# Unread matmuls in TensorE's waits, and another order around the end of the second attention

## The chip, the cores and the metric

The kernel runs on one NeuronCore of a Trainium2 chip. The metric is the time of one execution on the device, in microseconds (us). Five engines work from their own instruction lists and wait for one another through semaphores: TensorE (PE, matrix products; its weight loads are listed apart as PEld), VectorE (DVE), ScalarE (ACT), GpSimd (POOL) and SyncE (SP, which here only starts transfers). TensorE's results go to PSUM, eight banks of 128 x 512 float32 numbers, from which VectorE and ScalarE read them.

## What is computed

Eight sequences of 128 tokens with 128 features pass through two layers. Each layer has a cross-attention to a context of the same shape and a feed-forward part, both added to the running x; each normalises its input.

```python
# layer 0: cross-attention, 16 heads of 8, with relative positions
energy = q k^T + q rel^T;  attn = softmax(energy / sqrt(8));  x += (attn v) Wo + bo
# layer 0: feed-forward with fake-quantised activations and weights (352 hidden)
xq = quant(ln(x)); h = quant(silu(xq Wg^T) * (xq Wu^T)); x += h Wd^T
# layer 1: cross-attention, 16 heads of 8
probs = softmax(q k^T / sqrt(8));  x += (probs v) Wo^T + bo
# layer 1: feed-forward, itself two blocks ("local layers") on z = ln(x)
h = shift_token(z); q, k, v = split(h @ wqkv)            # 8 heads of 64
q, k = rotary_xpos(l2norm(q) * qs, l2norm(k) * ks)
z += local_attention(q, k, v) @ wo                       # masked, window of 64
h = ln(shift_token(z)); a, g = split(h @ w1 + b1); z += (a * gelu(g)) @ w2 + b2
out = x + z
```

Here `shift_token` moves the upper 64 features one token on.

## The kernel before

Everything stays on the chip: 8 tiles of 128 tokens (n = 0 to 7), one per sequence. Each engine's program is a Python function that writes instructions in a fixed order; nothing reorders them later. So an instruction that waits for a semaphore holds back all that stands behind it on its engine.

**End of the first feed-forward part.** `spread_max(1)` (TensorE, L432 and L434) spreads the largest hidden value. VectorE scales and rounds the hidden values (L881, L883), ScalarE writes them as bf16 `hq` (L1334), and TensorE multiplies them by the down weights (L453) in two halves of four tiles. VectorE adds the result to x (`add_feed_forward(c)`, L1049 and L1053), takes mean and variance (`moments`, L770 to L775), and after a logarithm and an exponential on ScalarE (`norm_root`) three steps of Newton and the rows Y (`normalise`, L788 to L783). TensorE's `queries1(h)` turns four rows (L462) and projects them (L465).

**Second attention.** It runs in 16 units u, two per tile, each with eight heads. TensorE: `scores1` (L478, in PSUM banks 0 to 3), `turn1` (transposes of the probabilities, L491), `weigh1` (L503). VectorE: maximum (L1077) and subtraction (L1081). ScalarE: exponential (L1444) and two copies of the turned probabilities (L1441). After two units ScalarE takes the weighed values (`take_batch`), TensorE turns them back (`turn_back`, L517, bank 7) and VectorE divides them (`divide_batch`, L1068 and L1070). For each half of four tiles TensorE turns the outputs and projects them (`turn_second_o` L292, `project_second_o` L298), VectorE adds them to x (`add_projection(1, h)`, L866) and takes moments. Then z is normalised into `Z`, turned by TensorE (`turn_z(h)`, L525, bank 7) and copied into the shifted `hT` by ScalarE (L1347, L1348).

**Local layers.** A loop of 16 passes, one per tile and layer, that is started while the attention ends. `qkv(i)` (L549) makes queries, keys and values as three matmuls in banks 0, 1 and 2, with one semaphore at the end. ScalarE squares (L1361) and copies values (L1366). VectorE's `rotate(i)` (L1105 to L1117) applies the rotary tables and sums the squares, `unit_norm(i)` scales (to L1123). TensorE's `turn_qk` (L562), `score` and `shift` (both through L251: band and scores, then the negative maximum), `turn_p` (L607), `weigh` (L616), `turn_o` (L591) and `project_o` (L597) follow. VectorE's `largest(i)` (L1130) gives the maximum, ScalarE's `exponential(i)` (L1390) the probabilities.

The semaphores that carry the work around the change are `less_max` (subtraction done), `exp1`, `z_in` (rows of z), `zT` (`hT` filled), `rope` (turned queries and keys scaled), `kT`, `lmax`, `lexp`.

## Time and profile before

| | |
|---|---|
| three runs | 458.27, 458.41, 460.68 us (median 458.41) |
| profiled execution, its own time | 460.31 us |
| its span, first to last instruction | 458.5 us |
| mean granted clock of TensorE | 0.918 of 2.4 GHz |
| busy: TensorE, VectorE, ScalarE | 382.0, 356.7, 235.5 us |

Busy shares alone do not say what a stage waits for. In the timeline a row is a start, a duration, an engine with its line, what it writes and reads, how many instructions are merged, and in brackets how long the engine had been idle and what ended that. The clock is either 1.2 or 2.4 GHz (0.50 or 1.00 of full); a stretch with a number between contains both.

### The profile page before, as it was taken

The numbers are of one execution on the slowest core, as the hardware profiler recorded it, in microseconds if no ns is written. First come the engines' busy times: TensorE is split into PE (matmuls) and PEld (weight loads), VectorE is DVE, ScalarE is ACT, GpSimd is POOL, SyncE is SP. The second block draws the span as 40 slices with busy tenths as digits, with TensorE's granted clock in tenths as the row PEclk, the third lists the DMA queues.
The fourth block names the chain that finished last, engine by engine and source line by source line (L and its number), as shares of the span: only waits on it lengthen the run. The fifth ranks groups of instructions, "written<-read, shape, count | busy, mean of one in ns | idle before, by whom it ended". The sixth has DMA issues, their size and how long they took to land.

```text
span 458.5 us, 10020 instructions
## 1 busy us (share of the span) xinstructions
PE 382.0 (83%) x4101; PEld 280.6 (61%) x4101; DVE 356.7 (78%) x721; ACT 235.5 (51%) x432; POOL 21.0 (5%) x30
## 2 busy tenths in 40 slices
PE   3898899998453689988777998999999899997966
PEld 1597788876312235554455676867767676776854
DVE  5999998997798679775877779878796978774542
ACT  1744444442454157765443455747656565754541
POOL 2000020000020110000000000000000001010110
PEclk9999999999755579997888999999999999997997
DMA  8500000000000000000000000000000000000000
GB/s 338 249 5 3 20 21 4 3 4 1 0 0 2 0 0 1 2 1 0 1 1 1 0 1 1 2 1 0 1 0 2 1 1 1 1 0 2 24 1 23
DMA packets 1773, 8.29 MB, mean 18 GB/s; under 512 B 192, under 2 KB 448, under 8 KB 1472
## 3 DMA queue, kind: packets, MB, share of 16 engines
q1 hardware_dynamic: 1728, 7.65, 4.2%
q8 instruction: 33, 0.54, 0.5%
q14 instruction: 12, 0.10, 0.1%
HBM read 7.12 MB, written 0.52 MB: 17 GB/s over the span
## 4 chain that ended last, share of the span: by engine, by line
PE 51%; DVE 33%; ACT 10%; issue 5%; DMA 1%; DVEq 0%; ACTq 0%
PE ps L251 12%; PE ps L549 9%; DVE blk L825 5%; PE ps L649 5%; PE ps L616 3%; PE ps L661 3%; PE ps L491 2%; PE ps L478 2%; PE ps L607 2%; DVE blk L1114 2%; DVE blk L1105 2%; PE ps L597 2%; DVE ss L1115 2%; ACT blk L1361 2%; ACT PT L1444 2%
## 5 line engine op out<-in xcount | busy, mean ns | idle before, releaser
L549 PE MATMUL ps<-w_f,full 128*128 128x512 f32 x96 | 45.8, 614 | 0.7 <-DVE blk L1109 0.7
L1293 ACT ACTIVATE St<-ps 128x512 bf16<-128x512 f32 x32 | 19.1, 597 | 44.9 <-PE ps L251 44.9
L1105 DVE TENSOR_TENSOR blk<-ps,tabs 128x1024 f32<-128x1024 f32 x16 | 19.6, 1224 | 28.9 <-ACT blk L1361 28.9
L1361 ACT ACTIVATE blk<-ps 128x1024 f32<-128x1024 f32 x16 | 16.4, 1027 | 30.5 <-PE ps L549 30.5
L616 PEld LDWEIGHTS ps<-blk,PT 128*128 128x128 f32 x256 | 30.3, 192 | 1.6
L616 PE MATMUL ps<-blk,PT 128*128 128x65 f32 x256 | 31.3, 275 | 0.0
L549 PEld LDWEIGHTS ps<-w_f,full 128*128 128x128 f32 x96 | 18.5, 200 | 18.8 <-issue 17.7
L251 PEld LDWEIGHTS ps<-blk,st 128*128 128x128 bf16 x768 | 26.7, 98 | 3.8
L251 PE MATMUL ps<-blk,rel 128*128 128x64 bf16 x768 | 27.6, 193 | 0.0
L251 PE MATMUL ps<-blk,st 128*128 128x64 bf16 x768 | 27.6, 193 | 0.0
L607 PE MATMUL ps<-const,PT 128*128 128x128 f32 x128 | 17.9, 285 | 9.3 <-ACT blk L1384 9.3
L1390 ACT ACTIVATE PT<-ps 128x1024 f32<-128x1024 f32 x16 | 16.3, 1019 | 17.3 <-PE ps L251 17.3
L649 PE MATMUL ps<-YT,w_f 128*128 128x256 f32 (+1 forms) x96 | 24.5, 408 | 0.7 <-ACT YT L1414 0.7
L966 DVE TENSOR_REDUCE mneg<-ps 128x4 bf16<-128x512 bf16 x32 | 22.0, 686 | 3.5 <-PE ps L349 3.3
L251 PEld LDWEIGHTS ps<-blk,rel 128*128 128x128 bf16 x768 | 24.6, 98 | 0.0
L562 PEld LDWEIGHTS ps<-const,blk 128*128 128x128 f32 x128 | 16.2, 151 | 12.9 <-DVE blk L1123 7.6
L491 PEld LDWEIGHTS ps<-const,PT 128*128 128x128 f32 x128 | 14.3, 144 | 15.4 <-ACT PT L1444 14.1
L1441 ACT ACTIVATE PT<-ps 128x512 f32<-128x512 f32 x32 | 17.5, 596 | 10.6 <-PE ps L491 10.5
L1077 DVE TENSOR_REDUCE m<-ps 128x8 f32<-128x1024 f32 x16 | 19.5, 1221 | 4.1 <-PE ps L478 4.0
L478 PE MATMUL ps<-blk,full 64*128 64x512 f32 x64 | 20.4, 726 | 2.7 <-DVE PT L1081 1.9
L607 PEld LDWEIGHTS ps<-const,PT 128*128 128x128 f32 x128 | 14.5, 146 | 12.6 <-issue 12.6
L562 PE MATMUL ps<-const,blk 128*128 128x128 f32 x128 | 18.4, 292 | 4.1 <-DVE blk L1123 4.1
(231 smaller groups left out, 886.4 us busy)
## 6 DMA issues: line engine op xcount, KB each, us to landing
w_f<-f_dram SPq DMA_DIRECT2D x2, 1689.0 KB, 13.2
w_x<-l_dram SPq DMA_DIRECT2D x1, 774.0 KB, 5.9
w_f<-ffn_dram SPq DMA_DIRECT2D x1, 561.0 KB, 7.9
X<-x_dram SPq DMA_DIRECT2D x1, 512.0 KB, 3.5
ctxT<-ctxT_dram SPq DMA_DIRECT2D x1, 512.0 KB, 4.4
OT<-maskT_dram SPq DMA_DIRECT2D x1, 512.0 KB, 7.0
rest<-l_dram SPq DMA_DIRECT2D x1, 385.0 KB, 5.0
const<-const_dram SPq DMA_DIRECT2D x1, 324.0 KB, 6.2
```

What stands on the lines that cost most here:

```text
L251: return mm(out, l, r, start=start, stop=False, skip_group_check=True)
L478: i = mm(ps[:, 2 * c + g, :].rearrange("p (h k) -> p h k", h=4), full[r:r + 64, 2, P * n:P * (n + 1)], kblk[r:r + 64, 4 * c:4 * c + 4, n, ...
L491: i = tr(ps[:, 4 + c, P * j:P * (j + 1)], S1[:, u % 2, P * (4 * c + j):P * (4 * c + j + 1)], ident)
L549: m = mm(ps[:, c, :], hT[:, n, :], w_f[:, l, F_QKV + 512 * c:F_QKV + 512 * (c + 1)], start=True, stop=True)
L562: t = tr(ps[:, 5 + c, P * j:P * (j + 1)], R[:, i % 2, P * (4 * c + j):P * (4 * c + j + 1)], ident)
L607: t = tr(ps[:, 5 + c, P * j:P * (j + 1)], S1[:, i % 2, P * (4 * c + j):P * (4 * c + j + 1)], ident)
L616: m = mm(ps[:, 5 + h // 4, 65 * (h % 4):65 * (h % 4 + 1)], P1[:, i % 2, P * h:P * (h + 1)], VL[:, i % 3, s, :], start=(h % 4 == 0), stop=T ...
L649: x = mm(ps[0:r, t, 256 * m:256 * (m + 1)], w_f[:, l, F_W1 + HID * m + P * t:F_W1 + HID * m + P * t + r], YT[:, 256 * j:256 * (j + 1)], st ...
L825: v.tensor_tensor(ring[:, c % RING, :, :, :, :].rearrange("p b n q h -> p (b n) q h"), src.to_broadcast([P, 2 * NB, QC, HG]), keep.to_broa ...
L966: v.tensor_reduce(mneg[:, c % 2, :], turned_b[:, c % 2, :].rearrange("p (j k) -> p j k", j=4), AX.X, ALU.max).then_inc(sem("chunk_max"), 1)
L1105: step(v.tensor_tensor(heads(R[:, i % 2, :]), u, tab[:, 0].to_broadcast([P, 2, LH, LD]), ALU.mult))
L1361: a(SQ, ps[:, 0:2, :].rearrange("p b c -> p (b c)"), ACT.Square).then_inc(sem("squared"), 1)
```

## The change

It has four parts.

1. A new function `unread(n, bank)` issues n matmuls of 128x512 bf16 into a PSUM bank whose contents nobody reads afterwards. There are seven such groups, 37 matmuls in all: at the end of the feed-forward part (9, 2, 10, 3 and 2) and between the attention and the local layers (8 and 3).
2. At the end of the feed-forward part, VectorE normalises the first half before it adds the second half's result.
3. Around the end of the second attention: the addition of the first half's projection moves from behind unit 12 to behind unit 13; the rows of z are turned in front of `weigh1(13)`; the divisions of batches 5 to 7 and the whole second half (turn, projection, addition, moments, rows of z and their turn) come later, inside the first two passes of the loop. The second half of z is turned in bank 4 instead of 7. `score(0)` and `qkv(2)` go ahead of `turn_back(7)`.
4. The first tile's queries and keys are computed, signalled (`qk_ps`) and squared before its values (`v_tile_ps`).

```diff
+            def unread(n, bank):
+                for k in range(n):
+                    mm(ps[:, bank, :], ident_b[:, :], rel3[:, 0, :, :].rearrange("p g c -> p (g c)"), start=True, stop=True)
...
             spread_max(1)
+            unread(9, 0)
             for n in range(NB):
                 if n % 4 == 0:
+                    if n == 4:
+                        unread(2, 0)
                     pe.wait_ge(sem("hq"), 3 * (n // 4 + 1))
...
+                if h == 0:
+                    unread(3, 0)
                 pe.wait_ge(sem("yT"), 5 + h)
...
+            def turn_second_z():
+                pe.wait_ge(sem("lexp"), 2)
+                for n in range(4, NB):
+                    pe.wait_ge(sem("z_in"), n + 1)
+                    i = tr(ps[:, 4, (n % 4) * P:(n % 4 + 1) * P], Z[:, n, :], ident)
                 i.then_inc(sem("zT_ps"), 1)
...
-            def qkv(i):
+            def qkv(i, lo=0, hi=3):
...
-                    pe.wait_ge(sem("less_max"), G * NB)
+                    pe.wait_ge(sem("less_max"), G * NB - 1 if hi == 2 else G * NB)
...
-                for c in range(3):
+                for c in range(lo, hi):
                     m = mm(ps[:, c, :], hT[:, n, :], w_f[:, l, F_QKV + 512 * c:F_QKV + 512 * (c + 1)], start=True, stop=True)
-                m.then_inc(sem("qkv_ps"), 1)
+                    if c >= 1:
+                        m.then_inc(sem("qk_ps") if c == 1 else sem("v_tile_ps"), 1)
...
+            unread(10, 0)
             queries1(0)
+            unread(2, 0)
             scores1(0, 0)
...
             weigh1(2 * NB - 1)
             qkv(1)
+            unread(8, 4)
             turn_qk(0)
+            turn_back(6)
+            unread(3, 4)
+            score(0)
+            qkv(2)
             turn_back(7)
-            score(0)
-            turn_second_o(1)
-            project_second_o(1)
             for i in range(2 * NB):
                 shift(i)
...
+                if i == 0:
+                    turn_second_o(1)
+                if i == 1:
+                    turn_second_z()
...
                 turn_p(i)
+                if i == 0:
+                    project_second_o(1)
...
             add_feed_forward(0)
             moments(3, X, 0, 4)
+            normalise(3, X, Y, "y", 0, 4)
             add_feed_forward(1)
-            normalise(3, X, Y, "y", 0, 4)
...
-                if u == 12:
+                if u == 13:
                     add_projection(1, 0)
                     moments(5, X, 0, 4)
+                    divide_batch(4)
...
             rotate(0)
+            unit_norm(0)
+            divide_batch(5)
+            rotate(1)
             divide_batch(6)
-            unit_norm(0)
-            rotate(1)
-            divide_batch(7)
             unit_norm(1)
...
+                if u == 15:
+                    act.wait_ge(sem("h_zeroed"), 1)
+                    take_turned_z(0)
                 if u < U:
                     act.wait_ge(sem("less_max"), u + 1)
```

What this does to the order, at the places that matter. TensorE at the end of the feed-forward part, before: the spread of the maximum, 24 matmuls of the down projection, the turn of the rows and the query projection.

```order
L434 MATMUL ps<-gmax,ones 128x1
L453 MATMUL ps<-wdT,PT 128x128 x24
L462 MATMUL ps<-const,Y 128x128 x4
L465 MATMUL ps<-YT,rest 128x512
L478 MATMUL ps<-blk,full 128x512 x4
```

The same place now (L431 is the unread matmul, with the relative positions `rel3` as its moving operand):

```order
L438 MATMUL ps<-gmax,ones 128x1
L431 MATMUL ps<-rel,ident_b 128x512 x9
L460 MATMUL ps<-wdT,PT 128x128 x12
L431 MATMUL ps<-rel,ident_b 128x512 x2
L460 MATMUL ps<-wdT,PT 128x128 x12
L431 MATMUL ps<-rel,ident_b 128x512 x10
L469 MATMUL ps<-const,Y 128x128 x4
L431 MATMUL ps<-rel,ident_b 128x512 x3
L474 MATMUL ps<-YT,rest 128x512
L431 MATMUL ps<-rel,ident_b 128x512 x2
L487 MATMUL ps<-blk,full 128x512 x4
```

Five groups stand in front of five waits; each must end before what stands behind it can start. On VectorE at the end of the second attention, before, from the subtraction of unit 12 to that of unit 14:

```order
L1081 TENSOR_TENSOR PT<-ps,m 128x1024
L866 TENSOR_TENSOR X<-ps,X 128x512
L770 BN_STATS stats<-X 128x6 x4
L773 BN_AGGR mv<-stats 128x2 x4
L775 TENSOR_SCALAR ve<-mv 128x4
L1077 TENSOR_REDUCE m<-ps 128x8
L1081 TENSOR_TENSOR PT<-ps,m 128x1024
L1068 RECIPROCAL rec<-ps 128x16
L1070 TENSOR_TENSOR O<-ps,rec 128x8x2x8
L788 TENSOR_TENSOR nt<-r 128x4
```

Now, from the same subtraction (L1107 and L1111 are the maximum and the subtraction):

```order
L1111 TENSOR_TENSOR PT<-ps,m 128x1024
L1107 TENSOR_REDUCE m<-ps 128x8
L1111 TENSOR_TENSOR PT<-ps,m 128x1024
L896 TENSOR_TENSOR X<-ps,X 128x512
L800 BN_STATS stats<-X 128x6 x4
L803 BN_AGGR mv<-stats 128x2 x4
L805 TENSOR_SCALAR ve<-mv 128x4
L1098 RECIPROCAL rec<-ps 128x16
L1100 TENSOR_TENSOR O<-ps,rec 128x8x2x8
L1107 TENSOR_REDUCE m<-ps 128x8
L1111 TENSOR_TENSOR PT<-ps,m 128x1024
L818 TENSOR_TENSOR nt<-r 128x4
```

Unit 13 now passes the addition of the projection, and unit 14 the normalisation of z. On TensorE between the attention and the local layers, before, from the second group of three `qkv` matmuls to the first shift:

```order
L549 MATMUL ps<-w_f,full 128x512 x3
L562 MATMUL ps<-const,blk 128x128 x8
L517 MATMUL ps<-const,full 128x128 x2
L251 MATMUL ps<-band_b,ident_b 128x512 x2
L251 MATMUL ps<-blk 128x128 x8
L292 MATMUL ps<-const,O 128x128 x4
L298 MATMUL ps<-rest,OT 128x128 x4
L251 MATMUL ps<-lneg,ident_b 128x512 x2
```

Now, from the same `qkv` group to the same shift:

```order
L564 MATMUL ps<-w_f,full 128x512 x3
L431 MATMUL ps<-rel,ident_b 128x512 x8
L578 MATMUL ps<-const,blk 128x128 x8
L526 MATMUL ps<-const,full 128x128 x2
L431 MATMUL ps<-rel,ident_b 128x512 x3
L251 MATMUL ps<-band_b,ident_b 128x512 x2
L251 MATMUL ps<-blk 128x128 x8
L564 MATMUL ps<-w_f,full 128x512 x3
L526 MATMUL ps<-const,full 128x128 x2
L251 MATMUL ps<-lneg,ident_b 128x512 x2
```

The turn and projection of the second output half (L292, L298) have left the stretch ahead of the first shift, and the third `qkv` group has come in.

## Rows read from the trace of the kernel before

**Rows 1.** Page, part 2: granted clock, 40 slices of 11.5 us, tenths of full speed.

```profile
PEclk9999999999755579997888999999999999997997
```

**Rows 2.** Windows: stretch, us, busy us of PE, PEld, DVE, ACT, POOL, clock, DMA.

```profile
120.00:165.00 45.00, 25.07 (x74) 10.26 (x74) 35.79 (x95) 18.19 (x30) 7.58 (x10) 0.51 0.00 1
...
166.00:203.00 37.00, 36.05 (x363) 20.81 (x361) 30.80 (x41) 27.42 (x44) 0.00 (x0) 1.00 0.01 2
...
262.00:414.00 152.00, 140.78 (x988) 108.25 (x986) 122.38 (x240) 92.58 (x181) 5.67 (x8) 1.00 0.00 1
```

**Rows 3.** Timeline, end of the feed-forward part: start, us, engine, line, operation.

```profile
139.59 0.58 PE L434 MATMUL ps<-gmax,ones 1*128 1x1 f32 x2 [0.37 <-DVE gmax L1013]
...
144.13 1.46 PE L453 MATMUL ps<-wdT,PT 128*128 128x128 bf16 x12 [3.96 <-ACT PT L1334]
...
146.70 1.46 PE L453 MATMUL ps<-wdT,PT 128*128 128x128 bf16 x12 [1.10 <-ACT PT L1334]
...
148.62 0.17 DVE L775 TENSOR_SCALAR ve<-mv 128x4 f32<-128x4 f32 x1
...
149.48 0.69 DVE L1053 TENSOR_TENSOR X<-St,X 128x512 f32<-128x512 f32 x1
...
151.20 1.25 PE L462 MATMUL ps<-const,Y 128*128 128x128 f32 x4 [3.05 <-DVE Y L783]
...
155.99 3.79 PE L478 MATMUL ps<-blk,full 64*128 64x512 f32 x8 [0.78 <-ACT full L1341]
...
156.96 1.12 DVE L783 TENSOR_SCALAR Y<-X,mv,rstd 128x128 f32<-128x128 f32 x4
...
161.50 2.07 PE L465 MATMUL ps<-YT,rest 128*128 128x512 f32 x2 [0.69 <-ACT YT L1339]
...
165.43 1.10 PE L491 MATMUL ps<-const,PT 128*128 128x128 f32 x8
```

**Rows 4.** Timeline, TensorE: bf16 matmuls of 512 columns, slow and fast.

```profile
128.40 1.89 PE L445 MATMUL ps<-PT,wqT 128*128 128x512 bf16 x4 [2.25 <-ACT PT L1319]
...
235.54 0.60 PE L251 MATMUL ps<-lneg,ident_b 128*128 128x512 bf16 x2
```

**Rows 5.** Timeline, end of the second attention and the first passes.

```profile
196.31 1.13 PE L478 MATMUL ps<-blk,full 64*128 64x512 f32 x4
...
200.22 0.69 DVE L866 TENSOR_TENSOR X<-ps,X 128x512 f32<-128x512 f32 x1 [1.67 <-PE ps L298]
...
204.86 1.06 ACT L1444 ACTIVATE PT<-PT 128x1024 f32<-128x1024 f32 x1 [1.98 <-DVE PT L1081]
...
204.88 1.13 PE L478 MATMUL ps<-blk,full 64*128 64x512 f32 x4 [1.90 <-DVE PT L1081]
...
205.97 1.75 PE L491 MATMUL ps<-const,PT 128*128 128x128 f32 x8
...
211.60 1.10 PE L491 MATMUL ps<-const,PT 128*128 128x128 f32 x8 [1.83 <-ACT PT L1444]
...
214.11 4.00 PE L549 MATMUL ps<-w_f,full 128*128 128x512 f32 x6
...
219.27 1.22 DVE L1105 TENSOR_TENSOR blk<-ps,tabs 128x1024 f32<-128x1024 f32 x1 [5.45 <-ACT blk L1361]
...
224.18 0.17 DVE L1117 TENSOR_SCALAR ss<-ss 128x16 f32<-128x16 f32 x1
...
226.79 1.97 PE L562 MATMUL ps<-const,blk 128*128 128x128 f32 x8 [2.14 <-DVE blk L1123]
...
247.70 1.03 PE L251 MATMUL ps<-lneg,ident_b 128*128 128x512 bf16 x2 [2.29 <-DVE lneg L1130]
...
260.30 0.61 PE L251 MATMUL ps<-lneg,ident_b 128*128 128x512 bf16 x2
...
260.75 2.73 PE L549 MATMUL ps<-w_f,full 128*128 128x512 f32 x6
```

**Rows 6.** Page, part 5: VectorE's maximum in the second attention.

```profile
L1077 DVE TENSOR_REDUCE m<-ps 128x8 f32<-128x1024 f32 x16 | 19.5, 1221 | 4.1 <-PE ps L478 4.0
```

More of the change, by code:

```diff
@@ L518, in turn_back, with turn_first_z @@
                 i.then_inc(sem("o_back"), 1)
-            def turn_z(h):
-                if h == 0:
-                    pe.wait_ge(sem("o_norm"), 9)
-                for n in range(4 * h, 4 * h + 4):
+            def turn_first_z():
+                pe.wait_ge(sem("o_norm"), 9)
+                for n in range(4):
                     pe.wait_ge(sem("z_in"), n + 1)
-                    i = tr(ps[:, 7, (n % 4) * P:(n % 4 + 1) * P], Z[:, n, :], ident)
+                    i = tr(ps[:, 7, n * P:(n + 1) * P], Z[:, n, :], ident)
+                i.then_inc(sem("zT_ps"), 1)
+            def turn_second_z():
[3 more added lines that the diff above has]
+                    i = tr(ps[:, 4, (n % 4) * P:(n % 4 + 1) * P], Z[:, n, :], ident)
                 i.then_inc(sem("zT_ps"), 1)
@@ L588, in turn_o @@
                 else:
-                    pe.wait_ge(sem("zT"), 2)
+                    pe.wait_ge(sem("res_added"), 6)
                 for j in range(4):
@@ L673, in _ @@
                 turn1(2 * n)
-                if n >= 6:
-                    turn_back(n - 2)
+                if n == 6:
+                    turn_back(4)
+                if n == 7:
+                    turn_first_z()
                 if n >= 1:
@@ L681, in _ @@
                     pe.wait_ge(sem("f_in"), 32)
-                    qkv(0)
+                    qkv(0, 0, 2)
                 if n + 1 < NB:
@@ L685, in _ @@
                 turn1(2 * n + 1)
+                if n == 7:
+                    qkv(0, 2, 3)
                 weigh1(2 * n)
@@ L688, in _ @@
                     project_second_o(0)
-                if n == 6:
-                    turn_z(0)
-                if 1 <= n <= 4 or n == 7:
+                if n == 7:
+                    turn_back(5)
+                if 1 <= n <= 4:
                     turn_back(n - 1)
@@ L728, in _ @@
                         pe.wait_ge(sem("yT"), 7 + (i - 4) // 2)
+                    if i == 1:
+                        pe.wait_ge(sem("zT"), 2)
                     if 5 <= i <= 11 and i % 2 == 1:
@@ L1090, in _ @@
                     divide_batch(3)
-                if u == 13:
+                elif u == 14:
                     normalise(5, X, Z, "z_in", 0, 4)
@@ L1182, in _ @@
                 if i == 0:
-                    add_projection(1, 1)
-                    moments(6, X, 4, NB)
+                    divide_batch(7)
                 if i >= 5 and i % 2 == 1:
@@ L1194, in _ @@
                     quarter_rows((i - 4) // 2)
+                if i == 1:
+                    normalise(6, X, Z, "z_in", 4, NB)
                 if i + 2 < 2 * NB:
@@ L1197, in _ @@
                 if i == 0:
-                    normalise(6, X, Z, "z_in", 4, NB)
+                    add_projection(1, 1)
+                    moments(6, X, 4, NB)
                 if i >= 3 and i % 2 == 1:
@@ L1345, in take_turned_z @@
                 act.wait_ge(sem("zT_ps"), h + 1)
-                z = ps[:, 7, :].rearrange("p (n t) -> p n t", n=4)
+                z = ps[:, (7, 4)[h], :].rearrange("p (n t) -> p n t", n=4)
                 step(a(hT[0:64, 4 * h:4 * h + 4, :], z[0:64], ACT.Copy))
@@ L1357, in square @@
             def square(i):
-                act.wait_ge(sem("qkv_ps"), i + 1)
+                act.wait_ge(sem("qk_ps"), i + 1)
                 if i >= 1:
@@ L1363, in take_v @@
             def take_v(i):
+                act.wait_ge(sem("v_tile_ps"), i + 1)
                 if i >= 3:
@@ L1441, in _ @@
                         a(P1[:, w % 2, 512 * c:512 * (c + 1)], ps[:, 4 + c, :], ACT.Copy).then_inc(sem("pt1"), 1)
+                if u == 14:
+                    norm_root(5)
+                if u == 15:
+                    act.wait_ge(sem("h_zeroed"), 1)
+                    take_turned_z(0)
                 if u < U:
@@ L1456, in _ @@
                     square(0)
+                if u == 16:
                     take_v(0)
+            take_batch(7)
             head_root(0)
-            take_batch(7)
             square(1)
@@ L1463, in _ @@
             head_root(1)
-            take_output(1, 1)
             for i in range(2 * NB):
@@ L1468, in _ @@
                 exponential(i)
-                if i == 0:
+                if i == 1:
                     norm_root(6)
-                if i == 1:
-                    take_turned_z(1)
                 if i + 2 < 2 * NB:
@@ L1476, in _ @@
                     take_turned_qk(i + 1)
+                if i == 0:
+                    take_output(1, 1)
+                if i == 1:
+                    take_turned_z(1)
                 if i >= 3 and i % 2 == 1:
```

11 lines of the change are left out of this document (2 added, 9 removed).

## Prediction

> **What bounds the kernel now.** I read the page first: its clock line is at full rate except from about 120 to 170 us, in a ragged stretch from 200 to 250 us, and near the end [rows 1]. The windows give this in numbers: a granted clock of 0.51 over 120 to 165 us (1.2 GHz nearly throughout), 1.00 over 166 to 203 us and 1.00 over 262 to 414 us [rows 2]. The reader should see that the two places where the change works are the two where the clock is low or ragged. Then I read the timeline at the end of the feed-forward part [rows 3]: TensorE waits 3.96 us for the quantised hidden values, 1.10 us for their second half, 3.05 us for the normalised rows, and then works at 1.2 GHz until 165.4 us. Last I read the end of the second attention [rows 5]: VectorE waits 1.67 us for the projection while a unit of scores (its matmuls began at 196.31 and took 1.13 us) stands behind that wait, and TensorE then waits 1.90, 1.83, 2.14 and 2.29 us.
>
> Times below are those of the profiled execution. Its span is 458.5 us and its own time 460.31, so 1.8 us lie around it; the median of the three runs is 458.41, and the sum is taken off that. The three runs spread over 2.4 us.
>
> **Step 1, what an unread matmul costs.** 37 are added, each a bf16 128x512. No trace row is an unread one; the nearest have the same shape: four in 1.89 us at 1.2 GHz, two in 0.60 us at 2.4 GHz [rows 4]. Less a tail of about 0.17 us after the last, that is 0.43 us each slow and 0.215 fast. Bounds for all 37: 0 if each lies in a wait, 37 x 0.43 = 15.9 us if none does. They can't gain by themselves, only through the clock. In the feed-forward end: nine start when the second spread ends, at 139.59+0.58 = 140.2, and take 9 x 0.43 = 3.9 us, to 144.0; the work behind them is released at 144.1. Two more fill 145.6 to 146.5, before 146.7. The ten start at 148.2 or sooner. At 2.4 GHz they take 2.15 us and end at 150.3 at the latest; at 1.2 GHz they take 4.3 and end at 152.5. So the waits hide all of these if the clock is up by 148 us.
>
> Is it? Before, the clock rose at about 165 us (the turns at 165.43 already run at full rate), after TensorE had worked without a break since 161.50 [rows 3]. With the fillers TensorE works from 139.6 to 148.2 with at most a few tenths idle, more than twice as long. I take it as up at 148.
>
> **Step 2, the feed-forward end.** The variance of the first half is ready at 148.79 [rows 3]. Now the normalisation stands ahead of the second half's feed-forward addition, which held VectorE until 150.2. The root on ScalarE ends at 149.3, Newton's three steps take 0.6, four rows 1.1: rows from 149.9 to 151.1 rather than 150.8 to 151.9. From there: the turn ends at 151.4, ScalarE's copy at 152.05, the query projection at 2.4 GHz takes 1.0 (a third of a 2.73 us group of three of this size [rows 5], and its tail) instead of 2.07, copy to 153.9, scores in pairs of 1.13 us [rows 5] instead of 3.79 for four matmuls at 1.2 GHz [rows 3]: both units at 156.1. VectorE meanwhile adds, takes moments, and has the second half's rows ready at 156.3, where they ended at 158.1 before. It then reduces and subtracts the first unit (2 x 1.22 us, [rows 6]) until 158.75. ScalarE, after the second query copy, ends the exponential at 160.1. The first turn of probabilities starts at about 160.2, against 165.43 before [rows 3]. **Term A: -5.2 us.** From there until 200 us TensorE is nearly gapless (36.05 of 37 us [rows 2]), and its order there is kept, so the term is carried on.
>
> **Step 3, the end of the second attention** (times on the clock of before). VectorE's wait of 1.67 us at 200.22 began at 198.55; now unit 13 is reduced there, and its subtraction ends at 201.1 instead of 204.8. The addition and moments follow to 203.4, division of batch 4 to 203.9, unit 14 to 206.4 (before 210.5, the exponential's 1.06 us ahead of the turn at 211.60). TensorE: scores of unit 15 at 203.0, turn of unit 13 at 204.05, weighing to 205.65, then a wait of 1.9 for the exponential of unit 14 (1.06 us, [rows 5]) until 207.55. Rows of z are ready at 208.1, turned at 209.2, copied at 210.4. Queries and keys alone (two of the three matmuls, 1.8 us) end at 212.2, where all three ended at 218.1. ScalarE's exponential of unit 15 and the square follow; the rotation starts at 213.3 instead of 219.27. The values' matmul, taken out of this path, costs its 0.9 us after the turn of unit 15, where VectorE and ScalarE are what is waited for.
>
> From the rotation on VectorE is the bound: rotation and sum 5.05 us (219.27 to 224.35), root and scaling 2.4 (until the turn is released at 226.79), a division 0.55, the second rotation 5.05, division 0.55, scaling 1.9, maximum 1.2. That is 230.2 for the first shift against 235.54 [rows 4], so -5.3. The eight and three fillers there (2.4 us together) lie in TensorE's wait for the scaled queries, 218.5 to 220.8, and for the turned ones; slow, they would end at 222, with some 4 us of slack.
>
> Next the second output half. Before it stood ahead of the first shift and ahead of the third rotation. Now: exponential 230.8 to 231.9, square to 232.9, rotation 232.95 to 238.05, then addition and moments (2.2) to 240.25, maximum to 241.5: second shift at 241.5 against 247.70. In the next pass the second half of z and the queries of block 3 share ScalarE (1.15 us for the z copies, which now stand behind the key copies), the score waits for nothing more than before, and the third shift comes at 253.4 against 260.30: -6.9. From there both run the same loop (about 10.75 us a pass), limited mostly by TensorE.
>
> Against this stands the clock. Each of the four waits of 1.83 to 2.29 us above [rows 5] was followed by a fall to 1.2 GHz, and my schedule has a wait of 1.9 at 205.65 and one of 2.4 before the first shift. A fall after the former slows the turns (+1.4 until z is copied) and part of the two matmuls (+0.7; before, three took 4.00 instead of 2.73): +2.1. After the latter, most work waits for ScalarE; +0.5 to +1.0. I take one costly fall: **term B: -6.9 + 2.1 = -4.8 us.** Bounds: -6.9 to about 0.
>
> **Sum:** 458.4 - 5.2 - 4.8 = **448.4 us**. After 262 us nothing is changed, but the phase in which the clock falls near the end is open; the spread of the runs, about 2 us, prices that.
>
> **Rivals.**
> 1. *No costly fall in B:* 458.4 - 5.2 - 6.9 = 446.3. For it: the fillers and the shorter waits; against it: rows 5 have no wait of 1.8 us without a fall.
> 2. *B's gain is eaten:* falls after both waits, and passes that stand behind ScalarE, which now has exponential, square, two key copies and the output copy in a row. B is then -2: 451.2.
> 3. *The clock rises, but turns don't hold it.* Then all after 150 us runs at 1.2 GHz again: projection 152.9 to 155.0, scores to 159.5 against 159.78, so A is -0.3: 458.4 - 0.3 - 4.8 = 453.3. Against it: from 166 to 203 us turns (L491) are about a third of the work and the clock stays at 1.00 [rows 2]; and eight of them take 1.10 us at full rate, 1.75 where it falls [rows 3, 5]. The Trainium skill says, in "TensorE: Matmul & The Clock Gate", Part 4, that the full rate does not engage for transposes, since they do not count as work in the same way. By that rule this rival would be the forecast; the trace does not bear the first half of it out.
> 4. *The unread matmuls hold up the queue, slower than before.* If they don't lift the clock, each costs 0.43 us, and the ten end at 152.5 instead of 150.3. Then turn 153.7, projection 155.1 to 157.1, scores 157.9 to 161.7, first turn of probabilities 167.3: +1.9. In B at 1.2 GHz: queries and keys 3.4 us, the values 1.7, the next three 5.1, eight fillers 3.4, so the first shift comes at 237.7: +2.2. Together 462.5. It decides from where one takes over 0.21 us, since the ten then pass the first row. For it: 155.99 to 160.8 was gapless and did not lift the clock; against it: the stretch with fillers is nearly twice as long.
>
> **Chances.** Forecast 0.45 (its own range 447 to 450.5), rival 1 0.20, rival 2 0.17, rival 3 or a late clock in A 0.09, rival 4 0.05, otherwise 0.04. The range 444 to 453.5 reaches below rival 1 by the spread of the end, and up to rival 3. A difference within 0.5% (2.3 us) is about what a measurement can't tell from none: faster 0.91, within 0.04, slower 0.05.
>
> **What would show it.** A granted clock near 1.00 from 148 us on, rows of Y turned from about 150 us, the first turn of probabilities near 160 (A). If A is right and the third shift is about 10 us earlier than 260.3, B is right as well; the granted clock around 200 to 210 us tells rival 1 from the forecast, a wait of TensorE for ScalarE's key copies rival 2. A clock of 0.5 at 150 us, or fillers of 0.43 us that end after 151 us, would prove the forecast wrong.

## The result and the profile after

The changed kernel took 442.35 us (median of four runs, 440.03 to 443.62) against 458.54 us for the kernel before (four runs, 458.27 to 460.68). The ratio is 0.9635, with a 95% interval of 0.9601 to 0.9668. By the medians that is 16.2 us less, by the ratio 3.6%. The forecast was 448.4 us with a range of 444 to 453.5, so the direction was right and the size too small, outside the range. Timed again beside other kernels it took 442.24 us (six runs, 440.03 to 443.37; 0.9634, 0.9607 to 0.9662). Two runs stand far from all others and are left out everywhere below: one of 1258 us in the last experiment and one of 741 us of the kernel before.

The two profiled executions are 20.3 us apart in span (458.5 and 438.2 us), more than the medians, since they happened to catch a run of 460.31 us of the one and of 440.03 us of the other, the fastest time of the changed kernel's ten runs. The clock line of the page of after, against [rows 1], (40 slices, here of 11.0 us) shows two low slices where there were five in the first stretch, and one where there were four in the second:

```profile
PEclk9999999999955999999979999999999999998989
```

The windows (stretch, its us, busy us of PE, PEld, DVE, ACT and POOL, granted clock, DMA), against [rows 2]:

```profile
120.00:165.00 45.00, 30.43 (x138) 12.87 (x140) 39.64 (x101) 21.64 (x36) 7.58 (x10) 0.74 0.00 1
...
161.00:198.00 37.00, 36.07 (x366) 20.90 (x364) 32.99 (x43) 27.45 (x45) 0.19 (x1) 1.00 0.01 2
...
248.00:396.00 148.00, 140.09 (x988) 107.86 (x986) 123.18 (x242) 95.70 (x182) 7.43 (x8) 1.00 0.01 1
```

The mean clock over 120 to 165 us is 0.74 instead of 0.51. Where the clock rises and falls is read here and below from windows of 1 us: one with a number between 0.50 and 1.00 contains the change. The rise after:

```profile
142.00:143.00 1.00, 1.00 (x4) 0.38 (x3) 0.97 (x3) 0.87 (x2) 0.00 (x0) 0.50 0.02 8
143.00:144.00 1.00, 1.00 (x4) 0.22 (x2) 0.96 (x3) 0.87 (x2) 0.00 (x0) 0.77 0.00 0
144.00:145.00 1.00, 0.59 (x11) 0.60 (x12) 0.94 (x3) 0.86 (x2) 0.00 (x0) 1.00 0.00 0
```

and before:

```profile
164.00:165.00 1.00, 1.00 (x4) 0.01 (x2) 0.00 (x0) 1.00 (x2) 0.00 (x0) 0.50 0.00 0
165.00:166.00 1.00, 1.00 (x7) 0.58 (x6) 0.45 (x1) 0.25 (x1) 0.00 (x0) 0.86 0.00 0
```

The end of the feed-forward part in the timeline of after, against [rows 3]:

```profile
140.38 3.62 PE L431 MATMUL ps<-rel,ident_b 128*128 128x512 bf16 x9
...
144.41 0.86 PE L460 MATMUL ps<-wdT,PT 128*128 128x128 bf16 x12 [0.41 <-ACT PT L1367]
...
145.10 0.59 PE L431 MATMUL ps<-rel,ident_b 128*128 128x512 bf16 x2
...
147.67 2.32 PE L431 MATMUL ps<-rel,ident_b 128*128 128x512 bf16 x10
...
150.65 1.10 PE L469 MATMUL ps<-const,Y 128*128 128x128 f32 x4 [0.66 <-DVE Y L813]
...
154.34 1.99 PE L487 MATMUL ps<-blk,full 64*128 64x512 f32 x8 [0.35 <-ACT full L1374]
...
155.45 1.11 DVE L813 TENSOR_SCALAR Y<-X,mv,rstd 128x128 f32<-128x128 f32 x4
...
160.48 1.09 PE L500 MATMUL ps<-const,PT 128*128 128x128 f32 x8 [0.34 <-ACT PT L1483]
```

The nine unread matmuls ("fillers" from here on, L431) run at 1.2 GHz but for the last two, since the clock rises at about 143.5, and end at 144.0; the ten end at 150.0, just ahead of the first row of Y. The four score matmuls take 1.99 us instead of 3.79, and the first turn of probabilities (L500) comes at 160.48 instead of 165.43. The end of the second attention and the first passes, against [rows 5]:

```profile
195.91 0.68 DVE L896 TENSOR_TENSOR X<-ps,X 128x512 f32<-128x512 f32 x1
...
202.13 1.09 PE L500 MATMUL ps<-const,PT 128*128 128x128 f32 x8 [1.46 <-ACT PT L1483]
...
205.09 1.96 PE L564 MATMUL ps<-w_f,full 128*128 128x512 f32 x4 [0.87 <-issue]
...
208.20 1.23 DVE L1136 TENSOR_TENSOR blk<-ps,tabs 128x1024 f32<-128x1024 f32 x1 [2.87 <-ACT blk L1394]
...
213.42 1.89 PE L431 MATMUL ps<-rel,ident_b 128*128 128x512 bf16 x8
...
215.73 1.09 PE L578 MATMUL ps<-const,blk 128*128 128x128 f32 x8 [0.42 <-DVE blk L1154]
...
224.73 0.61 PE L251 MATMUL ps<-lneg,ident_b 128*128 128x512 bf16 x2 [2.05 <-DVE lneg L1161]
...
235.74 0.61 PE L251 MATMUL ps<-lneg,ident_b 128*128 128x512 bf16 x2
...
247.12 0.60 PE L251 MATMUL ps<-lneg,ident_b 128*128 128x512 bf16 x2
```

VectorE no longer waits ahead of the addition (195.91). TensorE's wait for the exponential of unit 14 is 1.46 us. The first tile's queries and keys are started at 205.09 and VectorE's rotation of them (L1136) at 208.20. The first three shifts come at 224.73, 235.74 and 247.12 instead of 235.54, 247.70 and 260.30.

Where the 20.3 us of the two profiles lie, by marks that both have (a shift is the last TensorE step of a pass ahead of its exponential, L251 with `lneg`, and there are 16):

| stretch | before | after | difference |
|---|---|---|---|
| start to first turn of probabilities | 165.43 | 160.48 | -4.95 |
| from there to the third shift | 94.87 | 86.64 | -8.2 |
| third to fifteenth shift (12 passes) | 153.20 | 149.08 | -4.1 |
| fifteenth shift to the end | 45.0 | 42.0 | -3.0 |

The fifteenth shift, before and after:

```profile
413.50 0.61 PE L251 MATMUL ps<-lneg,ident_b 128*128 128x512 bf16 x2 [0.85 <-DVE lneg L1130]
```

```profile
396.20 0.61 PE L251 MATMUL ps<-lneg,ident_b 128*128 128x512 bf16 x2
```

The third line of the table is the surprise: a stretch for which the prediction allowed nothing. One pass there, before: the three matmuls of `qkv`, ScalarE's square and VectorE's rotation.

```profile
283.12 2.73 PE L549 MATMUL ps<-w_f,full 128*128 128x512 f32 x6
...
285.89 1.03 ACT L1361 ACTIVATE blk<-ps 128x1024 f32<-128x1024 f32 x1 [1.55 <-PE ps L549]
...
286.95 1.22 DVE L1105 TENSOR_TENSOR blk<-ps,tabs 128x1024 f32<-128x1024 f32 x1 [0.63 <-ACT blk L1361]
```

And the same pass after:

```profile
268.95 2.73 PE L564 MATMUL ps<-w_f,full 128*128 128x512 f32 x6
...
270.87 1.02 ACT L1394 ACTIVATE blk<-ps 128x1024 f32<-128x1024 f32 x1 [0.69 <-PE ps L564]
...
272.15 1.22 DVE L1136 TENSOR_TENSOR blk<-ps,tabs 128x1024 f32<-128x1024 f32 x1
```

The square starts 1.9 us behind the start of the matmuls instead of 2.8, since it no longer waits for the values, and the rotation 3.2 instead of 3.8. Over the 12 passes VectorE waited for ScalarE's square 18.1 us before (waits: engine, line, releaser, us in total, times, longest):

```profile
DVE blk L1105 <- ACT blk L1361: 18.1, 12, 2.4
```

and TensorE in turn for VectorE's maximum:

```profile
PE ps L251 <- DVE lneg L1130: 2.1, 5, 0.8
```

After, VectorE's wait is less than half, and TensorE has none for the maximum left:

```profile
DVE blk L1136 <- ACT blk L1394: 8.6, 7, 1.5
```

This wait shrank by 9.5 us and the stretch by only 4.1. One reason is in the same view: VectorE now waits longer for TensorE's weighed values, before and after:

```profile
DVE lrec L1143 <- PE ps L616: 2.3, 5, 0.5
```

```profile
DVE lrec L1174 <- PE ps L632: 6.7, 10, 0.8
```

### The profile page after: what moved, and what is told of

It reads as the page before. It is cut to its first block, busy times and chain, and to the rows that moved or that the text cites. A ratio compares the mean times of both kernels' runs of the same rounds, so it can differ in the third digit from the quotient of the medians.

```text
span 438.2 us, 10109 instructions
## 1 busy us (share of the span) xinstructions
PE 378.0 (86%) x4138; PEld 277.6 (63%) x4138; DVE 357.0 (81%) x721; ACT 237.9 (54%) x432; POOL 22.8 (5%) x30
## 4 chain that ended last, share of the span: by engine, by line
PE 58%; DVE 25%; ACT 9%; issue 6%; DMA 1%; SPq 0%; ACTq 0%; DVEq 0%
PE ps L251 13%; PE ps L564 8%; PE ps L632 6%; DVE blk L855 5%; PE ps L665 4%; PE ps L613 3%; PE ps L500 3%; PE ps L578 3%; PE ps L677 3%; PE ps L623 2%; PE ps L487 2%; ACT PT L1483 2%; PE ps L263 2%; DVE mneg L996 2%; DMA w_x<-l_dram 1%
## 5 line engine op out<-in xcount | busy, mean ns | idle before, releaser
L564 PE MATMUL ps<-w_f,full 128*128 128x512 f32 x96 | 44.3, 594 | 1.4 <-issue 0.9
L1136 DVE TENSOR_TENSOR blk<-ps,tabs 128x1024 f32<-128x1024 f32 x16 | 19.5, 1221 | 13.7 <-ACT blk L1394 13.7
L251 PEld LDWEIGHTS ps<-blk,st 128*128 128x128 bf16 x768 | 26.7, 98 | 3.8
L564 PEld LDWEIGHTS ps<-w_f,full 128*128 128x128 f32 x96 | 17.5, 190 | 18.0 <-issue 16.8
L251 PE MATMUL ps<-blk,rel 128*128 128x64 bf16 x768 | 27.6, 193 | 0.0
L251 PE MATMUL ps<-blk,st 128*128 128x64 bf16 x768 | 27.6, 193 | 0.0
L251 PEld LDWEIGHTS ps<-blk,rel 128*128 128x128 bf16 x768 | 24.6, 98 | 0.0
L665 PE MATMUL ps<-YT,w_f 128*128 128x256 f32 (+1 forms) x96 | 23.6, 397 | 0.7 <-ACT YT L1448 0.7
L500 PEld LDWEIGHTS ps<-const,PT 128*128 128x128 f32 x128 | 13.8, 141 | 14.6 <-ACT PT L1483 13.6
L578 PEld LDWEIGHTS ps<-const,blk 128*128 128x128 f32 x128 | 15.1, 146 | 11.1 <-DVE blk L1154 7.8
L1145 DVE TENSOR_TENSOR blk<-blk 128x1024 f32<-128x1024 f32 x16 | 19.9, 1244 | 1.7
L855 DVE TENSOR_TENSOR blk<-blk,const 128x1024 bf16<-128x1024 bf16 x16 | 20.9, 1309 | 0.0
L1161 DVE TENSOR_REDUCE lneg<-ps 128x8 bf16<-128x1024 f32 x16 | 19.5, 1217 | 1.6 <-PE ps L251 1.4
```

Source lines behind the costliest of these rows:

```text
L251: return mm(out, l, r, start=start, stop=False, skip_group_check=True)
L500: i = tr(ps[:, 4 + c, P * j:P * (j + 1)], S1[:, u % 2, P * (4 * c + j):P * (4 * c + j + 1)], ident)
L564: m = mm(ps[:, c, :], hT[:, n, :], w_f[:, l, F_QKV + 512 * c:F_QKV + 512 * (c + 1)], start=True, stop=True)
L578: t = tr(ps[:, 5 + c, P * j:P * (j + 1)], R[:, i % 2, P * (4 * c + j):P * (4 * c + j + 1)], ident)
L665: x = mm(ps[0:r, t, 256 * m:256 * (m + 1)], w_f[:, l, F_W1 + HID * m + P * t:F_W1 + HID * m + P * t + r], YT[:, 256 * j:256 * (j + 1)], st ...
L855: v.tensor_tensor(ring[:, c % RING, :, :, :, :].rearrange("p b n q h -> p (b n) q h"), src.to_broadcast([P, 2 * NB, QC, HG]), keep.to_broa ...
```

## The experiments

The kernel before took 458.5 to 458.9 us beside each group of them. "First turn" is that of probabilities, in the profile of each.

| kernel | median us | runs' span | ratio to before, interval | first turn | third shift |
|---|---|---|---|---|---|
| changed, again | 442.24 | 440.03-443.37 | 0.9634 (0.9607-0.9662) | 160.45 | 247.09 |
| changed, no fillers | 443.00 | 442.83-444.64 | 0.9670 (0.9644-0.9696) | 163.95 | 252.12 |
| changed, late signals | 447.39 | 445.94-448.27 | 0.9756 (0.9731-0.9781) | 160.41 | 247.07 |
| before, early signals only | 451.18 | 450.81-456.71 | 0.9873 (0.9830-0.9916) | 164.00 | 257.43 |
| orders only | 449.97 | 446.48-451.25 | 0.9804 (0.9770-0.9839) | 164.46 | 252.51 |
| orders, first tile whole | 452.80 | 451.56-454.11 | 0.9891 (0.9865-0.9917) | 164.23 | 254.22 |
| before, unit 13 first | 455.83 | 453.86-457.52 | 0.9942 (0.9915-0.9970) | 163.91 | 256.50 |
| before, front fillers | 455.92 | 455.29-457.24 | 0.9933 (0.9907-0.9960) | 161.26 | 257.21 |
| before, rows sooner | 458.60 | 455.98-459.85 | 0.9985 (0.9967-1.0003) | 163.88 | 258.73 |
| before, both front edits | 454.59 | 453.47-456.08 | 0.9906 (0.9881-0.9931) | 160.34 | 256.19 |

### The signal for queries and keys in every tile

Theory 1: the prediction missed that `qkv` signals queries and keys after two matmuls in all 16 tiles, not only the first. The edit takes that back for tiles 1 to 15:

```diff
...
                 for c in range(lo, hi):
...
-                    if c >= 1:
+                    if i == 0 and c >= 1:
                         m.then_inc(sem("qk_ps") if c == 1 else sem("v_tile_ps"), 1)
+                if i >= 1:
+                    m.then_inc(sem("qk_ps"), 1)
...
```

> The changed kernel, but in tiles 1 to 15 of the local layers queries and keys are signalled only after the values' matmul, as before; the first tile keeps its early signal. Theory 1 (the step my prediction missed: the early signal lets ScalarE square and VectorE rotate 0.9 us sooner in every pass, about 4 us over passes 3 to 14 and about 1 in the first three): 442.4 + 5 = 447.5 us, pairs of passes 26.2 us long again instead of 25.6. Rival (those 4 us come from how the loop is entered, or from the clock): 442.5 us, pairs stay at 25.6.

Measured: 447.39 us, 5.15 above the changed kernel, as theory 1 had it (447.5). The third shift comes at 247.07, as with the early signals, so nothing of this was gained in the first three passes. Two shifts of its timeline, two passes apart:

```profile
282.64 0.60 PE L251 MATMUL ps<-lneg,ident_b 128*128 128x512 bf16 x2
...
308.80 0.60 PE L251 MATMUL ps<-lneg,ident_b 128*128 128x512 bf16 x2
```

Two passes last 26.16 us. The same two in the changed kernel last 25.61:

```profile
281.66 0.60 PE L251 MATMUL ps<-lneg,ident_b 128*128 128x512 bf16 x2
...
307.27 0.60 PE L251 MATMUL ps<-lneg,ident_b 128*128 128x512 bf16 x2
```

The converse, the kernel before with nothing but the early signals (ScalarE's waits, not shown, follow):

```diff
...
-                m.then_inc(sem("qkv_ps"), 1)
+                    if c >= 1:
+                        m.then_inc(sem("qk_ps") if c == 1 else sem("v_tile_ps"), 1)
...
```

> The kernel before with one edit: every qkv group signals queries and keys after two matmuls and values after the third. Theory 1: pairs of passes 25.6 us instead of 26.2, some 4 us in the loop and up to 1.5 around its start: 458.5 - 5 = 453.5 us. Rival (the early signal is worth something only behind the new order): within 1 us of 458.5.

Measured: 451.18 us, 7.3 below the kernel before and 2.3 below the forecast, though two of its six runs took 455.3 and 456.7 us, with a mean clock of 0.914 to 0.917 instead of 0.924 to 0.928. Its pairs last 25.60 us too:

```profile
291.97 0.60 PE L251 MATMUL ps<-lneg,ident_b 128*128 128x512 bf16 x2
...
317.57 0.60 PE L251 MATMUL ps<-lneg,ident_b 128*128 128x512 bf16 x2
```

The rival, that the way into the loop or the clock shortens the passes, falls: the length of a pair follows this one edit in both kernels, with the clock at 1.00 in all of them. The other profiles agree: 25.6 us with the early signals and 26.2 without, whatever else they have. It is the largest of the pieces that were run alone.

### The orders around the end of the second attention

All orders of the change, but no fillers, the rows at their old place and late signals in tiles 1 to 15:

```diff
...
-            unread(9, 0)
...
-            unread(10, 0)
...
             moments(3, X, 0, 4)
-            normalise(3, X, Y, "y", 0, 4)
             add_feed_forward(1)
+            normalise(3, X, Y, "y", 0, 4)
...
```

(the other five groups and the signals alike).

> Only the orders around the end of the second attention and the first tile's early signal: no unread matmuls, normalisation at its old place, late signals in tiles 1 to 15. Theory 1 (my term B, up to -6.9 without a costly fall of the clock, -4.8 with one): 458.5 - 5.5 = 453 us, with the third shift at about 254.5 us against 260.3. Rival (term B comes from the fillers of 8 and 3 and from the early signals): at most -2, 456.5 us or more.

Measured: 449.97 us (446.48 to 451.25), so -8.5, more than theory 1's -5.5; the rival is out. The forecast's term B was -4.8, its bound -6.9. In the profile the third shift stands 88.05 us behind the first turn of probabilities instead of 94.87: -6.8, with a fall of the clock at 239.1 us in between. What else the two profiles differ by lies in front of the first turn (1.0 us) and behind the fifteenth shift (3.5 us), where the clock changed at other times, so part of the -8.5 may be the clock's. The next kernel goes on from there and makes the first tile's three matmuls one group again:

```diff
-                    qkv(0, 0, 2)
+                    qkv(0)
...
-                if n == 7:
-                    qkv(0, 2, 3)
```

> The orders alone, as in the run of 450.0 us, but the first tile's queries, keys and values are again three matmuls in a row ahead of the turn of unit 15, signalled at the end. Theory 1 (the early signal of the first tile saves its own 0.9 us and the wait for the last subtraction, about 2 to 3 us of the start of the rotation): 452.5 us. Rival (VectorE's order carries all of term B): 450 us.

Measured: 452.80 us (theory 1: 452.5). The first tile's early start is worth 2.8 us. And one order alone, on the kernel before:

```diff
-                if u == 12:
+                if u == 13:
                     add_projection(1, 0)
                     moments(5, X, 0, 4)
...
-                if u == 13:
+                if u == 14:
                     normalise(5, X, Z, "z_in", 0, 4)
```

> The kernel before with one edit: on VectorE, unit 13 passes the addition of the first projection and its moments, and unit 14 the rows of z. Theory 1 (VectorE's 1.67 us wait is filled, and the last units are ready about 2.4 us sooner): 456 us. Rival (the rows of z come later and hold back the turn of z, which stands ahead of unit 14's turn on TensorE): 458.5 us or more.

Measured: 455.83 us, -2.7 (theory 1: 456). The rows of z do come after unit 14, and TensorE turns them ahead of unit 14's probabilities, after a wait of 1.30 us:

```profile
205.41 1.00 PE L525 MATMUL ps<-const,zv 128*128 128x128 f32 x4 [1.30 <-DVE zv L783]
...
206.25 1.04 PE L491 MATMUL ps<-const,PT 128*128 128x128 f32 x8
```

but both are sooner than before (208.65 and 211.60), even when the 1.5 us are taken off by which this profile is ahead from the first turn on. So, if the pieces add up, the 8.5 us are 2.7 for unit 13, 2.8 for the first tile, and by subtraction 3.0 for the rest, the later second half among it. That rest was not run alone, and the interval of the 8.5 is 1.6 us to either side.

### The front: fillers and sooner rows

Without the 37 fillers:

```diff
...
-            unread(9, 0)
...
-            unread(10, 0)
...
-            unread(8, 4)
...
-            unread(3, 4)
...
```

(and the groups of 2, 3 and 2 alike).

> The changed kernel without any of the 37 unread matmuls; all orders as in the change. Theory 1 (the fillers lift the clock at the end of the feed-forward part, and the orders bring the rest): the clock is 0.50 again until about 165 us, the first turn of probabilities comes at about 164.5 us (rows sooner alone give about 0.5 to 1), the later gain stays; 442.4 + 4.5 = about 447 us. Rival (the orders at the front give the 5 us and the fillers only fill): first turn at 160.5 us, 442 us.

Measured: 443.00 us. In its profile the clock stays at 1.2 GHz until 160.4 us (143.5 with fillers), and the first scores take 3.79 us again:

```profile
160.00:161.00 1.00, 0.41 (x2) 0.01 (x1) 1.00 (x2) 0.55 (x1) 0.86 (x4) 0.81 0.00 0
```

```profile
155.58 3.79 PE L482 MATMUL ps<-blk,full 64*128 64x512 f32 x8 [0.78 <-ACT full L1365]
...
163.95 1.09 PE L495 MATMUL ps<-const,PT 128*128 128x128 f32 x8 [0.66 <-ACT PT L1474]
```

The first turn is 3.5 us later, as theory 1 had it, but the time is not 447: the median is only 0.8 us higher, and by the two ratios to the kernel before the fillers are worth 1.7 us. The changed kernel timed again, and the front's edits one by one on the kernel before:

> The changed kernel as it is, to time it beside the next three on one chip. 442.4 us as in its first four runs. If the fillers are worth their 3.5 us of the profiles (first turn of probabilities 160.48 with, 163.95 without), it lies at 440 to 442; the runs without fillers had 443.0, so if they are worth nothing it lies at 443.

> The kernel before plus the five groups of unread matmuls at the end of the feed-forward part (26), nothing else. Theory 1 (they lift the clock, and the stage was bound by TensorE at 1.2 GHz): first turn of probabilities at about 161 us instead of 165.4, time 458.5 - 4.5 = 454 us. Rival (they lift the clock, but it falls sooner later on, so that the gain is given back): first turn at 161, time 456 to 458 us. Rival 2 (they only fill): 165.4 and 458.5 us.

> The kernel before with one edit: VectorE normalises the first half before it adds the second half's feed-forward result. Theory 1 (at 1.2 GHz the stage is bound by TensorE from the first rows on, so all comes as much sooner as the rows do): first turn of probabilities 0.5 to 1.5 us sooner, 457.5 us. Rival (what counts is the second half's rows, which come no sooner): 458.5 us.

> Both edits of the feed-forward end on the kernel before, late signals and old orders elsewhere. Theory 1: my term A, first turn at 160.5 us and 458.5 - 5.2 = 453.3 us. Rival (gain given back by a clock that falls later): first turn at 160.5, time 455 us or more.

The edits of the last three are, in this order, the unread matmuls, the two moved lines at the end, and both:

```diff
...
+            unread(9, 0)
...
+                    if n == 4:
+                        unread(2, 0)
...
+                if h == 0:
+                    unread(3, 0)
...
+            unread(10, 0)
             queries1(0)
+            unread(2, 0)
...
             moments(3, X, 0, 4)
+            normalise(3, X, Y, "y", 0, 4)
             add_feed_forward(1)
-            normalise(3, X, Y, "y", 0, 4)
```

Fillers alone: 455.92 us, -2.7 (theory 1: -4.5), with the first turn at 161.26. Rows alone: 458.60, nothing, within 0.3%: the rival. Both: 454.59, -4.0 (theory 1: -5.2), with the first turn at 160.34. The sooner rows are worth something only with the fillers: nothing without them, 0.9 us at the first turn and 1.3 us in the medians with them, the latter within the noise. The expectations compared with a first turn at 165.4. Besides that of before there are seven profiles without front fillers, and in all of them it is at 163.4 to 164.5, because the clock rises near 160 us and not at 165 as in the one profile that the prediction had. Against 164.0 term A is -3.6.

The fillers ahead of the first scores:

> The changed kernel without the 8 and 3 unread matmuls ahead of the first scores; the 26 at the front stay. Theory 1 (they stand in waits and only keep the clock up; without them TensorE waits about 2.1 us there and the clock may fall): first shift at 224.7 us as with them if it doesn't fall, 442.5 us; up to 444 us where it falls. Rival (they cost time, since they hold back the turn of queries and keys): 441.5 us or less.

```diff
...
-            unread(8, 4)
...
-            unread(3, 4)
...
```

Measured: 442.39 us (440.98 to 445.37; 0.9648, 0.9616 to 0.9681), with the first shift at 224.70: no difference in time that can be measured, and no cost either. In its profile TensorE waited 2.14 us at that place and the clock fell at 218.1, and again at 235.1 us; the second shift was on time and the third 1.4 us late:

```profile
235.70 1.03 PE L251 MATMUL ps<-lneg,ident_b 128*128 128x512 bf16 x2 [1.89 <-DVE lneg L1159]
...
248.49 0.60 PE L251 MATMUL ps<-lneg,ident_b 128*128 128x512 bf16 x2
```

The other profiles bear this out. Count from the first turn to the third shift, in the kernels with all the new orders. Where a fall begins between 235 and 239 us it is 88.0 to 88.3 us: in the four without these fillers, and in one with them. In the six others, all with them, it is 86.6 to 86.7.

### The clock near the end

> The changed kernel plus six unread matmuls ahead of the turn of unit 14 (a wait of 1.46 us) and nine ahead of the first shift (a wait of 2.05 us, after which the clock fell from 225.4 to 232.2 us). Theory 1 (the fall costs little, most work there waits for ScalarE and VectorE): no fall, 0.5 to 1.5 us less, 441.3 us. Rival (the fall in the first two passes is what keeps the fillers from paying more): 439.5 us or less. A third way: they run past the wait and cost up to 0.5 us.

```diff
...
+                if n == 7:
+                    pe.wait_ge(sem("o_norm"), 9)
+                    unread(6, 7)
                 turn1(2 * n)
...
             turn_back(7)
+            unread(9, 5)
...
```

Measured: 441.23 us (439.57 to 445.14; 0.9641, 0.9595 to 0.9687). The fall at 225 us is gone, the third shift is at 247.05 as before: that fall had cost nothing. No gain in time can be told.

> The changed kernel plus unread matmuls in three waits near the end: nine behind the shift of pass 14 (2.14 us wait), ten ahead of the last but one down projection (2.16) and four ahead of the last (1.07). Theory 1 (the spread of 3.3 us between runs of one kernel is the clock falling or not after these waits): the runs lie closer together and near the best one, 440 us. Rival (the spread comes from elsewhere): median and spread as they were, 442.2 us and 3 us.

```diff
...
+                if i == 14:
+                    pe.wait_ge(sem("rotated"), 16)
+                    unread(9, 0)
                 if i + 1 < 2 * NB:
                     turn_qk(i + 1)
...
             hidden(16, 6)
+            unread(10, 4)
             down(17, 6)
...
             hidden(18, 7)
+            unread(4, 4)
             down(19, 7)
...
```

Measured: 439.57 us (438.69 to 441.62; 0.9582, 0.9554 to 0.9611), 2.7 below the changed kernel's median. Repeated:

> The changed kernel plus unread matmuls in three waits near the end, a second time. If the first result holds: 439.6 us, between 438.7 and 441.6. If it was luck of the clock: 441 to 442 us.

439.32 us (438.33 to 441.38; 0.9595, 0.9570 to 0.9621). **This beats both kernels of the case.** The changed kernel was timed in other groups, so the fairer comparison is that of the ratios to the kernel before: 0.9634 for it, 0.9582 and 0.9595 here, or 1.8 to 2.4 us. In the changed kernel the turn of queries and keys in pass 14 waited 2.14 us and took 1.52 us, as the clock fell during it:

```profile
398.94 1.52 PE L578 MATMUL ps<-const,blk 128*128 128x128 f32 x8 [2.14 <-DVE blk L1154]
```

With nine fillers in that wait, the wait is 0.20 us and the turn runs at full rate:

```profile
396.48 2.10 PE L431 MATMUL ps<-rel,ident_b 128*128 128x512 bf16 x9
...
398.78 1.09 PE L578 MATMUL ps<-const,blk 128*128 128x128 f32 x8 [0.20 <-DVE blk L1159]
```

The next shift, the sixteenth, comes at 408.98 instead of 410.12, so about 1 us of the gain is shown there:

```profile
410.12 0.60 PE L251 MATMUL ps<-lneg,ident_b 128*128 128x512 bf16 x2
```

```profile
408.98 0.60 PE L251 MATMUL ps<-lneg,ident_b 128*128 128x512 bf16 x2
```

Where the rest comes from is not shown. This profile's span, 438.5 us, is no shorter than the 438.2 of the changed kernel's, whose profile caught its fastest run.

The spread of the runs hardly fell (2.9 and 3.1 us instead of 3.3), so half of theory 1 is wrong: a fall a little later, at about 418 us, remains, in a stretch of short waits of 0.3 to 1.0 us, and lasts 6.8 us in the one profile and 3.4 in the other.

> Both sets of further unread matmuls on the changed kernel. Theory 1: the gains add up, 439 us, spread under 1.5 us. Rival: no better than with the tail's alone, 440 us, since in the middle the engines other than TensorE set the pace.

Both sets together: 439.94 us (439.07 to 441.21; 0.9590, 0.9561 to 0.9618), no better than the tail's alone: the rival. In its profile the fall at 225 us is gone again, but another came at 236.6 us, and the third shift at 248.60, 1.5 us late. The same fillers in the middle had no such fall in their own profile.

> The changed kernel without its 37 unread matmuls but with the 23 near the end. Theory 1 (front fillers are worth their 3.5 us of the profiles, and the clock near the end hid it in the comparison of medians): 439.6 + 3.5 = 443 us. Rival (the front's gain is really given back before the end): 440.4 us, 0.8 above the kernel with both.

The edit is that of the kernel without fillers together with the 23 near the end. Measured: 444.11 to 445.09 us in four runs (ratio 0.9708, 0.9683 to 0.9734), so 444.8, which is 5.5 above the repeat of the kernel with both and more than either expectation. The two profiles say where: 3.0 us at the first turn, 1.3 from there to the third shift, nothing over the twelve passes, and 1.3 behind the fifteenth shift. Between the plain pair the same 37 matmuls brought 0.8 us in the medians. Its profiles differ alike up to the third shift (3.5 and 1.5 us), but behind the fifteenth the kernel with fillers loses 0.4. So what the front's gain is worth hangs on where the falls near the end land; what moves them was not settled. How long TensorE waits is not enough to tell. In four kernels without the fillers of 8 and 3 it waited 2.14 or 2.15 us for the scaled queries, and the clock fell during the turn behind that wait or within 1.3 us of its end. In the kernel without any fillers it also waited 2.15 us there, and yet the turn ran at full rate and there was no fall before 228.6 us:

```profile
219.19 1.09 PE L573 MATMUL ps<-const,blk 128*128 128x128 f32 x8 [2.15 <-DVE blk L1145]
```

## Why the prediction was right and wrong

**Step 1, right.** Nine fillers took 3.62 us (forecast 3.9), the ten ended at 150.0 (150.3 at the latest). None held up its follower, and the clock was up by 148 us: at 143.5, and at 143.0 to 145.9 in the other profiles with these fillers. Rival 4 and rival 3 are out: after the rise eight turns took 1.09 us, against the 1.75 and 1.97 of [rows 5] where the clock was low. The Trainium skill ("TensorE: Matmul & The Clock Gate", Part 4) says that the full rate does not engage for transposes, since they do not count as work in the same way. These fp32 transposes ran at the full rate, so the first half of that does not hold here; whether they count for less no run tells.

**Step 2, right in the profile, too large as an effect.** The first turn was forecast at 160.2 and measured at 160.48. But the 165.43 it was compared with is late; against other profiles without fillers term A is -3.6, and -4.0 in time when made alone, instead of -5.2.

**Step 3, right in mechanism, too small.** On the clock of before (4.95 us added to the times of after) the rotation was forecast at 213.3 and came at 213.15, the first shift at 230.2 and came at 229.7, the second at 241.5 and came at 240.7, the third at 253.4 and came at 252.1. The term that failed is the +2.1 for "one costly fall": the wait of 1.9 us that should have brought it was 1.46, and no fall followed. The fall after the wait of 2.05 us did come (225.4 to 232.2 us) and cost nothing. So rival 1 described this stretch, and rival 2 did not come. The bound of -6.9, drawn up without a costly fall, was itself 1.3 us short: -8.2 in the profile, which has none. A costly fall can come in this stretch, but at another place and for less: the orders alone have one from 239.1 us on, and there it is -6.8. The prediction gave the fillers of 8 and 3 no gain here; the kernels without them all have such a fall, worth 1.4 us.

**The step that failed.** "From there both run the same loop" and "After 262 us nothing is changed". The diff changes `qkv`, which runs in all 16 tiles. The prediction used the early signal for the first tile only, and part 4 of the change names no more. The loop was also called "about 10.75 us a pass", which is the distance from the third to the fourth shift; over the twelve passes the mean was 12.8, and two passes took 26.2. The profile had what was needed: ScalarE's square waited for L549 in all 12 passes, and VectorE's rotation waited 18.1 us for the square. That stretch, put at nothing, was worth 4.1 us in the profiles, and the early signals 5.15 us (taken away) and 7.3 us (added alone) in time.

So two terms were too small, B by 3.4 us and the loop by 4.1, and A was too large by 1.2. The sum with what was measured is 458.4 - 4.0 - 8.2 - 4.1 = 442.1, against 442.35 measured. That it fits so closely is luck in part: the 4.0 is a difference of medians and the others are read from two profiles. The three pieces in time alone, 4.0, 8.5 and 5.15, would give 440.8.

**The end.** The 3.0 us that the two profiles differ behind the fifteenth shift (45.0 and 42.0) go with the clock. In the kernel before it was at 1.2 GHz over 414.5 to 421.3 and 445.2 to 452.0, in the changed one over 399.5 to 402.9, 419.9 to 423.4 and from 437.0 on. In the profiles of kernels with the signals of before this part took 41.5 to 45.3 us, so it is not what the change did. How much of the 3.0 is in the medians no run tells.

## What to carry to other kernels

When a diff edits a helper, list every place that calls it before calling any stretch unchanged; here the helper's loop held between a fifth of the gain (4.1 of 20.3 us, profiles) and a third (5.15 of 16.2, medians). Signal each result where its reader needs it: with one semaphore at the end of a group of three matmuls, VectorE waited 9.5 us longer for ScalarE over 12 passes. Matmuls that nobody reads were free in a wait here as long as they ended before the release, but their worth hangs on where the clock would fall later, so they are judged by several timed runs and not by one profile.

## What was unexpected of the hardware

TensorE's clock rose at 165 us in the one profile of before, and at 159.5 to 160.6 us in the seven other profiles without front fillers, four of which have the same instructions up to there. In those four the first turn of probabilities came at 163.9 to 164.5 instead of 165.4 us. Waits of 1.83 to 2.29 us were each followed by a fall in the kernel before, while one of 2.15 us in the kernel without fillers was not, and near the end a fall came in a stretch whose longest wait was 1.03 us. And what a fall costs depends on where it lies: with and without the one from 225.4 to 232.2 us the third shift came at 247.1 us, while one of half that length that began at 235 to 239 us made it 1.4 us late.
